# AdaLN block on one core: the out-projection in halves of 256 tokens, the MLP's first tile opened by its high parts, a table load and modulation columns placed otherwise

## What is computed

```
mod = silu(c) @ wmod          # six sets of columns: sa, ca, ga, sb, cb, gb
h = layernorm(x) * (1 + ca) + sa
x = x + ga * attention_block(h)   # RMS norm, q/k/v, rope, 32 heads of 8, causal softmax
                                  # inside blocks of 128 tokens, out-projection + residual,
                                  # RMS norm, silu(gate) * value, down-projection + residual
h = layernorm(x) * (1 + cb) + sb
x = x + gb * ffn(h)               # gated FFN of 704 with the top 2 of 8 LoRA experts
```

## Time and profile before

| | |
|---|---|
| profiled execution | 675.88 us |
| its span, first to last instruction | 674.0 us |
| PE busy | 627.5 us (93%) |
| PEld busy | 419.7 us (62%) |
| DVE busy | 408.1 us (61%) |
| ACT busy | 316.1 us (47%) |
| POOL busy | 196.5 us (29%) |
| mean granted TensorE clock | 0.968 of full |

### The profile page before, as it was taken

One profiled execution on the slowest core, in us unless ns is written; L12 is line 12 of the kernel. 1 busy time (PEld: TensorE's weight loads), 2 busy tenths in 40 slices (PEclk: granted clock), 3 DMA queues, 4 the chain that ended last, 5 costly groups with the idle time before them and its releaser, 6 DMA issues.

```text
span 674.0 us, 13925 instructions
## 1 busy us (share of the span) xinstructions
PE 627.5 (93%) x5784; PEld 419.7 (62%) x5784; DVE 408.1 (61%) x623; ACT 316.1 (47%) x478; POOL 196.5 (29%) x264
## 2 busy tenths in 40 slices
PE   5779999999999999999999998999999999969996
PEld 3645566577864666667774565766785565637772
DVE  2895644677467653668557564468647654447554
ACT  3736463356444355257444345437543544417441
POOL 1156640024016670033015662023103773000000
PEclk8689999999999999999999999999999999978997
DMA  8644000034022000025012100004102100000000
GB/s 329 227 121 132 3 3 1 1 79 110 1 62 94 2 2 2 1 51 138 1 32 64 63 3 2 1 14 123 53 1 63 64 2 2 1 0 1 1 2 31
DMA packets 16456, 31.77 MB, mean 47 GB/s; under 512 B 5060, under 2 KB 5828, under 8 KB 16260
## 3 DMA queue, kind: packets, MB, share of 16 engines
q1 hardware_dynamic: 14856, 27.98, 13.8%
q0 software_dynamic: 1152, 2.36, 1.3%
q10 hardware_dynamic: 384, 0.52, 0.3%
HBM read 12.99 MB, written 2.10 MB: 22 GB/s over the span
## 4 chain that ended last, share of the span: by engine, by line
PE 69%; DVE 13%; ACT 7%; SPq 4%; issue 4%; DMA 1%; POOL 0%; DVEq 0%; ACTq 0%; POOLq 0%
PE bank L1623 8%; PE bank L1533 7%; PE bank L1429 5%; PE bank L1425 5%; PE bank L1426 5%; SPq L409 4%; PE bank L1695 4%; PE bank L1561 3%; PE bank L1595 3%; PE bank L1790 3%; PE bank L1569 3%; PE bank L1792 3%; PE bank L1791 2%; PE bank L1659 2%; PE bank L1816 2%
## 5 line engine op out<-in xcount | busy, mean ns | idle before, releaser
L1142 DVE TENSOR_REDUCE neg_max<-bank 128x8 f32<-128x1024 f32 x64 | 77.6, 1223 | 45.7 <-PE bank L1561 45.2
L1332 DVE TENSOR_TENSOR arena<-arena,bank 128x512 f32<-128x512 f32 (+1 forms) x72 | 49.5, 688 | 72.5 <-ACT arena L864 70.7
L1425 PE MATMUL bank<-n_hi,w_lo 128*128 128x512 f32 x200 | 86.5, 433 | 6.4 <-ACT n_hi L829 3.0
L1533 PE MATMUL bank<-mask 128*128 128x512 bf16 x256 | 78.5, 389 | 5.0 <-ACT n_hi L679 2.2
L1429 PE MATMUL bank<-n_lo,w_hi 128*128 128x512 f32 x200 | 81.4, 407 | 0.7
L864 ACT ACTIVATE arena<-bank 128x512 f32<-128x512 f32 (+1 forms) x72 | 43.0, 597 | 82.7 <-PE bank L1792 47.7
L1426 PE MATMUL bank<-n_hi,w_hi 128*128 128x512 f32 x200 | 80.3, 402 | 0.0
L803 ACT ACTIVATE tile_f<-bank 128x1024 f32<-128x1024 f32 x56 | 57.2, 1025 | 32.6 <-PE bank L1595 32.0
L581 POOL TENSOR_SCALAR arena_r<-q_st,const 100x512 fp32r<-100x512 f32 x96 | 65.2, 693 | 0.0
L560 POOL TENSOR_TENSOR k_wide<-n_lo,head_of 128x512 fp32r<-128x512 f32 x30 | 32.4, 1084 | 104.9 <-DMA n_lo<-k_st 104.9
L534 POOL TENSOR_TENSOR tile_f<-tile_f,const 128x512 f32<-128x512 f32 x16 | 22.2, 1392 | 138.6 <-ACT tile_f L715 138.6
(11 more groups left out here) (177 smaller groups left out, 1182.2 us busy)
## 6 DMA issues: line engine op xcount, KB each, us to landing
q_st<-arena_r SPq DMA_DIRECT2D x96, 64.0 KB, 2.1
k_st<-arena_r SPq DMA_DIRECT2D x52, 64.0 KB, 2.0
k_st<-arena_r POOLq DMA_DIRECT2D x36, 64.0 KB, 2.3
h_next<-in_x SPq DMA_DIRECT2D x4, 512.0 KB, 3.7
tile_f<-in_x SPq DMA_DIRECT2D x4, 512.0 KB, 4.9
out<-arena SPq DMA_DIRECT2D x4, 512.0 KB, 2.6
n_lo<-k_st SPq DMA_DIRECT2D x24, 64.0 KB, 2.0
n_hi<-q_st SPq DMA_DIRECT2D x24, 64.0 KB, 2.0
```

Of the source, the lines that this page charges most:

```text
L1142: nc.vector.tensor_reduce(neg_max[:, 2 * a:2 * a + 2, MROW:KS], slot(("s1", n)).rearrange("p a (h s) -> p a h s", s=P), AX_X, ALU.max, neg ...
L1332: nc.vector.tensor_tensor(pair_tmp[n % 2][0:width], silu_out[n % 2][0:width], up, ALU.mult)\
L1425: nc.tensor.matmul(to, wl[:, at], n_hi[:, kt, :], start=kt == 0, stop=False)
L1533: nc.tensor.matmul(to, mask[:, 0, :], mask[:, which:which + 1, :].broadcast_to([P, GH, P]), start=True, stop=False)
```

## The change

The out-projection is done in two halves of 256 tokens, in the order tile 0 half 0, tile 0 half 1, tile 1 half 0, tile 1 half 1, with 16 instructions in four banks (0 and 1, then 2 and 5); the first two groups wait for units 0 to 3, the third for units 4 and 5, the last for all. VectorE adds in four pieces of 256 tokens. The next row's second squared means move behind the out-projection, and VectorE's `variance` behind the low parts; ScalarE's squares for the MLP wait for these means, since both use the same tile. The first `up` step takes all products with high inputs for both outputs first and then those with low inputs. ScalarE loads the Exp table at the end of the feed-forward part. The four spreads of the queries are all tensor_scalars. The copies of modulation columns go and all readers take their columns from `mod_all`. In the prologue VectorE takes the second unit's maxima before the last low rope, and GpSimd waits for that low rope before it begins unit 1.

```diff
-        mod = sb("mod", [P, 6 * KT])
-        front_mod = sb("front_mod", [P, 2 * KT])
+        begun = sb("begun", [P, 1])
...
-        o_proj = signal("o_proj", KT)
+        o_proj = signal("o_proj", 2 * KT)
...
+        def columns(row, c):
+            return mod_all[:, c * KT:(c + 1) * KT, row:row + 1].rearrange("p c b -> p (c b)")
+
+        def out_bank(half, t):
+            return bank[:, ((0, 1), (2, 5))[half][t], 0:S // 2]
@@ GpSimd: spread_queries and the prologue @@
-                nc.gpsimd.tensor_tensor(q_ex[u % 2][0:KS, :, 0, :], src,
-                                        con("head")[0:KS, 0:1].unsqueeze(2).broadcast_to([KS, GQ, P]), ALU.mult)
-                for hh in range(1, GH):
+                for hh in range(GH):
                     last = nc.gpsimd.tensor_scalar(q_ex[u % 2][0:KS, :, hh, :], src,
                                                   con("head")[0:KS, hh:hh + 1], 1.0, ALU.mult, ALU.mult)
...
             spread_keys(0, 2, 0)
+            pool.wait_ge(rope_lo.sem, 4)
             unit_begun(0, 1, 0)
@@ ScalarE: row_steps @@
+                if not last:
+                    act.wait_ge(front.square_mean.sem, front.square_mean.count(row, 2, 1))
                 squares(rest, 0, h)
                 deviation(rest, row, 0, 0)
...
                 product_high(len(FF_STEPS) - 1)
                 if not last:
+                    nc.scalar.preload_act_table(ACT.Exp)
                     for u in range(AHEAD):
                         max_to_rows(row, u, 1)
@@ VectorE: row_steps @@
-                nc.vector.tensor_copy(mod[:], mod_all[:, :, bass.ds(row, 1)].rearrange("p c b -> p (c b)"))\
-                    .then_inc(mod_row.sem, 1)
...
-                            front_modulation(row, 1)
...
-                if not is_last:
-                    variance(1, row)
 
                 dve.wait_ge(h_moved.sem, h_moved.count(row, 1))
-                for t in range(KT):
-                    dve.wait_ge(o_proj.sem, o_proj.count(row, t + 1))
-                    nc.vector.tensor_tensor(h[:, t, :], h[:, t, :], bank[:, t, :], ALU.add).then_inc(x1_ready.sem, 1)
+                for half in range(2):
+                    tokens = slice(half * S // 2, (half + 1) * S // 2)
+                    for t in range(KT):
+                        dve.wait_ge(o_proj.sem, o_proj.count(row, half * KT + t + 1))
+                        last = nc.vector.tensor_tensor(h[:, t, tokens], h[:, t, tokens], out_bank(half, t), ALU.add)
+                        if half:
+                            last.then_inc(x1_ready.sem, 1)
 
...
+                if not is_last:
+                    variance(1, row)
                 inverse(rest, row, 0, 0)
@@ VectorE: prologue @@
             second_keys()
+            unit_max(0, 1, 0)
             rope_low(0, 3, 0)
-            unit_max(0, 1, 0)
             chunk_low(2)
@@ TensorE: row_steps @@
-                        elif u == 7:
-                            mean_squares(front, row, 1, 1)
...
-                for kt in range(KT):
-                    pe.wait_ge(ctx_done.sem, ctx_done.count(row, (kt + 1) * BLOCKS))
+                for kt, units, half in ((0, BLOCKS, 0), (0, BLOCKS, 1), (1, BLOCKS + BLOCKS // 2, 0), (1, UNITS, 1)):
+                    pe.wait_ge(ctx_done.sem, ctx_done.count(row, units))
                     for t in range(KT):
-                        last = nc.tensor.matmul(bank[:, t, :], plain("o")[:, kt * D + t * P:kt * D + (t + 1) * P],
-                                                ctx_n[:, kt, :], start=kt == 0, stop=kt == KT - 1)
+                        last = nc.tensor.matmul(out_bank(half, t), plain("o")[:, kt * D + t * P:kt * D + (t + 1) * P],
+                                                ctx_n[:, kt, half * S // 2:(half + 1) * S // 2], start=kt == 0,
+                                                stop=kt == KT - 1)
                         if kt == KT - 1:
                             last.then_inc(o_proj.sem, 1)
+                if not is_last:
+                    mean_squares(front, row, 1, 1)
+
+                def first_up():
+                    wh, wl = hi_lo("up")
+                    at = [[slice(kt * 2 * INTER + part * INTER, kt * 2 * INTER + part * INTER + P)
+                           for part in range(2)] for kt in range(KT)]
+                    to = [bank[:, up_bank(0, part), :] for part in range(2)]
+                    for kt in range(KT):
+                        pe.wait_ge(rest.n_hi_ready.sem, rest.n_hi_ready.count(row, kt + 1))
+                        for part in range(2):
+                            nc.tensor.matmul(to[part], wl[:, at[kt][part]], n_hi[:, kt, :], start=kt == 0, stop=False,
+                                             skip_group_check=True)
+                            nc.tensor.matmul(to[part], wh[:, at[kt][part]], n_hi[:, kt, :], start=False, stop=False,
+                                             skip_group_check=True)
+                    for kt in range(KT):
+                        pe.wait_ge(rest.n_lo_ready.sem, rest.n_lo_ready.count(row, kt + 1))
+                        for part in range(2):
+                            last = nc.tensor.matmul(to[part], wh[:, at[kt][part]], n_lo[:, kt, :], start=False,
+                                                    stop=kt == KT - 1, skip_group_check=True)
+                    return last
```

More of the change, by code:

```diff
@@ L692, in deviation, with shift @@
                     .then_inc(norm.std_ready.sem, 1)
-            def shift(norm, row, ahead, to, src, columns):
+            def shift(norm, row, ahead, to, src, shifts):
                 for t in range(KT):
                     act.wait_ge(norm.scaled.sem, norm.scaled.count(row, t + 1, ahead))
-                    last = nc.scalar.activation(to[:, t, :], src[:, t, :], ACT.Identity, bias=columns[:, t:t + 1])
+                    last = nc.scalar.activation(to[:, t, :], src[:, t, :], ACT.Identity, bias=shifts[:, t:t + 1])
                 last.then_inc(norm.shifted.sem, 1)
@@ L705, in front_squares @@
                 else:
-                    shift(front, row, ahead, h_next, h_next, front_mod[:, 0:KT])
+                    shift(front, row, ahead, h_next, h_next, columns(row + ahead, 0))
                 squares(front, n, h_next)
@@ L735, in second_norm_highs @@
                     nc.scalar.activation(n_hi[:, t, :], xc[:, t, :], ACT.Identity,
-                                         bias=mod[:, 3 * KT + t:3 * KT + t + 1]).then_inc(rest.n_hi_ready.sem, 1)
+                                         bias=columns(row, 3)[:, t:t + 1]).then_inc(rest.n_hi_ready.sem, 1)
             def second_norm_shift(row):
@@ L742, in second_norm_shift @@
                     last = nc.scalar.activation(xc[:, t, :], xc[:, t, :], ACT.Identity,
-                                                bias=mod[:, 3 * KT + t:3 * KT + t + 1])
+                                                bias=columns(row, 3)[:, t:t + 1])
                 last.then_inc(rest.shifted.sem, 1)
@@ L1073, in variance @@
                     .then_inc(front.std_ready.sem, 1)
-            def front_modulation(row, ahead):
-                nc.vector.tensor_copy(front_mod[:], mod_all[:, 0:2 * KT, bass.ds(row + ahead, 1)]
-                                      .rearrange("p c b -> p (c b)")).then_inc(front_mod_ready.sem, 1)
             def front_scale(row, ahead):
-                dve.wait_ge(front_mod_ready.sem, front_mod_ready.count(row, 1, ahead))
-                scale(front, row, 0, ahead, h_next, h_next, front_mod[:, KT:2 * KT], front.scaled)
+                scale(front, row, 0, ahead, h_next, h_next, columns(row + ahead, 1), front.scaled)
             def front_rms(row, ahead):
@@ L1123, in front_rope @@
                 rope_add(row, 0, 1)
-                scale(rest, row, 1, 0, xc, xc, mod[:, 4 * KT:5 * KT], rest.scaled)
+                scale(rest, row, 1, 0, xc, xc, columns(row, 4), rest.scaled)
                 rope_low(row, 0, 1)
@@ L1383, in _ @@
             front_columns()
-            front_modulation(0, 0)
             inverse(front, 0, 0, 0)
```

30 lines of the change are left out of this document (13 added, 17 removed).

## The result

The changed kernel takes 665.65 us (median of four runs, 665.0 to 667.4), beside 675.59 us for the kernel before on the same chip: ratio 0.9864, 95% interval 0.9848 to 0.9880, or 9.9 us less by the medians and 9.2 by the ratio. Forecast were 4.8 to 5 us less (670.8, range 668.0 to 673.5). The sign was right; the size forecast was about half of the measured one, and one of the places, the feed-forward part, had been put at 0. The profiled execution took 665.03 us, its span is 663.2 us (674.0 before), its mean granted clock 0.978 (0.968).

The account below looks back on a forecast made before the run. TensorE sets the time (69% of the chain), except where a row's work passes singly through other engines. Junction 3.5 + row starts 0.75 + columns 0 + prologue 0.75 = 5.0 us off 675.9, stated as 670.8, range 668.0 to 673.5.

Parts of the forecast that it names:

- Columns in place: 0: Modulation columns read without copies: worth 0, with bounds of 0.3 us gained and 0.3 lost.
- Together 1.07 us in each of the three rows: Junction between attention and MLP, rows with a successor: 0.65 - 0.06 + 0.48 = 1.07 us gained in each.
- I take 0.25 a row: Start of three rows: Exp load ahead (0.13) and first spread as tensor_scalar (0.10); 0.75 us in all, bounds 0 and 1.2.
- the prologue's 0.75: Prologue: four tensor_scalar spreads save 0.39 us and the later low rope 0.38; 0.75 taken, bounds 0.4 and 1.3.
- the clock of the last row: Last row: moving everything some 5 us earlier can shift a low-clock stretch either way by 1 us; left unsigned.
- Mechanism of the junction: After attention: 16 instructions 0.231 us apart, statistic behind them, `up` pair 3.0 instead of 3.48; 3.5 us over four rows.
- Rival (c): Out-projection: exposed weight loads of 0.19 us on 16 instructions cost 10.6 us in all, giving 681.4, slower; 4%.
- The 0.65 by which the first x1 was to come earlier: Junction, row 0: first x1 tile ends at 104.87 instead of about 105.52, ScalarE's high parts earlier with it.
- the bound 0.4: Start of a row: upper bound of 0.4 us a row if the first scores also came earlier.
- rival (a): Prologue: clock returns to the higher level a step earlier, 1.7 us more gained, 669.1; 20%.
- (b): Downstream of the junction: its gain is taken back, in full 674.4 or half 672.6; 7% each.
- (d): Change not doing what it says: Exp load stays at row start or halves wait for all contexts; 671.5 to 673; 5%.

Follow-up runs that it names:

- e1: Kernel before with the junction's three edits alone (out-projection in halves, moved statistic, first `up` by high parts): 669.1 against 674.62 us, 0.9917.
- e5: Kernel before with the Exp table loaded ahead and all four query spreads as tensor_scalars, without the prologue's new order: 672.32 against 673.8 us, 0.9974.
- e6: Kernel before with the modulation columns read in place, nothing else: 673.0 against 673.8 us, 0.9984.
- e9: Kernel before with only the next row's second squared means moved behind the whole out-projection, first `up` order kept: 671.54 against 674.04 us, 0.9954.
- e10: Kernel after with the out-projection and its additions whole again: 665.3 us against 674.04 for the kernel before, 0.9865.
- e2: Kernel before with the four query spreads as tensor_scalars and the prologue's new order: 673.41 against 674.62 us, 0.9981.
- e3: Kernel before with only the Exp table loaded at the end of the feed-forward part: 674.57 against 674.62 us, 0.9998.
- e13: Kernel after with the two copies of modulation columns back: 665.75 us against 674.42 for the kernel before, 0.9869.
- e14: Kernel after with the out-projection whole and fill matmuls in the last row, 3 of them before the last down-projection: 662.48 against 674.42 us, 0.9822.
- the repeat: Kernel after, unchanged, profiled and timed again in another session: 665.45 us against 674.62 for the kernel before, 0.9868.
- the control: Kernel after with VectorE setting the fill tile at the start but no fill matmul: 666.47 us against 674.04 for the kernel before, 0.9886.

## Why the prediction was wrong in size

The steps that failed are terms of the sum. "Columns in place: 0", with nothing for the feed-forward part, measured 1.3 to 1.45 us there. "Together 1.07 us in each of the three rows" measured 2.06 in row 2. "I take 0.25 a row" measured 0.39, the prologue's 0.75 measured 1.26 and 2.31, and the clock of the last row, left out, gave 0.3 to 0.6. The runs with parts of the change say the same in times: by their ratios e1 gave 5.6 us (3.5 said), e5 1.8 (1.1 said for its parts, 0.75 and the 0.39 of the spreads) and e6 1.1 (0 said). They leave out only the prologue's order, and make 8.5 together beside the 8.9 to 9.2 of the whole.

- **Mechanism of the junction: right.** 0.228 us apart (0.231 said), pair 2.99 (3.0 said), rows 0 and 1 1.18 and 1.21 (1.07 said), last row 0.39 (0.30 said). The rule of the Trainium skill's page "TensorE: Matmul & The Clock Gate", section "Part 3: Packing small matmuls — row/col tiling", that loads to the same row group are exposed, does not hold here: 16 instructions with a load each took 3.72 us, eight took 3.67 to 3.70. The prediction left out that the same section also lets a load into the background weight buffer go ahead; which buffer a load went to, the traces do not show. Rival (c) falls.
- **Its parts were in the sum, under a heading that hid them.** The 0.65 by which the first x1 was to come earlier is 0.82 for the statistic moved away less 0.17 for the halves. By e9 and e10 the move is worth 0.80 and the halves -0.11, and the pair's order 0.46. So the sum itself said that the halves lose, and I did not draw from it that the out-projection should stay whole.
- **"Together 1.07 us in each of the three rows" failed in row 2.** I read row 0 and multiplied by three; row 2 held an interruption of 0.69 us. It gave 0.85 more than rows 0 and 1, 0.99 more than said. A look at each of the three rows of the kernel before would have shown it.
- **"I take 0.25 a row" failed: 0.39.** I priced the load at 0.13 and the spread at 0.10 as if they added. e2 and e3 show 0 and 0.12 each alone and e5 0.37 to 0.40 together; the bound 0.4 was in the text, for the earlier first scores, and that is what came.
- **"Columns in place: 0" failed:** I looked for a cost in the operations that read the columns and there is none, but matmuls of the feed-forward part are spaced 4 to 5 ns closer, 0.2 us a row (e6, e13). The bound of 0.3 in all was too narrow. The part as a whole gave 1.3 to 1.45. Row 0's rest is open: the profile before has a slow DMA issue of 1.54 us in SyncE's queue in it (157.69), but e10 and e14, with the columns in place, take 60.35 and 60.55 there.
- **The prologue term was right in its two parts, and too small for the whole.** The spreads became 0.90 shorter (0.77 said), and e2 and e5 lie 0.7 below the mean of the profiles without the edit. With the whole change it was 1.26 and 2.31. The rest of the scatter is the issue pause near 17 us, 1.41 before, 2.56 after, 1.34 in the repeat, which no edit aims at, and the clock: rival (a), the clock back sooner, came in both (0.92 and 1.00 where it was 0.50). It was priced at 1.7; in the repeat, whose pause is as long as before's, 1.56 beyond the 0.75 came. In e13 the clock is 1.00 in both stretches of the earlier trace rows and the pause 2.04, and the first contexts come at 53.32, 1.6 earlier than before.
- **The clock was left out of the sum as unsigned.** In the last row it gave 0.3 to 0.6, and at the end 1.8 or nothing, by the execution. So 1.3 + 0.4 + 1.4 + 0.5 (junction, row starts, feed-forward part, prologue) = 3.6 us are terms of mine that were too small, and the remaining 2.2 of the 5.8 by which the profiles differ more than my 5.0 are the last row and the tail. Of these the tail's 1.8 is chance: the repeat does not have it.
- **Rivals (b) and (d) did not come.** Nothing was given back: the marks only ever move apart. No table load stands before Exp in rows 1 to 3.
- The range failed because all unknowns were bounded one by one near their middle values, and four of them came out on one side.

## What to carry to other kernels

When a term is "so much a row", read the place in every row of the trace before, since one of three was different. When two waits end at nearly the same time, price them together; tests of one alone show little. And when an order is changed in several ways at once, test each: here the edit with the most code (the halves) was worth a loss of 0.11 us a row, while the move of one statistic made most of the junction's gain.

## What was not expected of the hardware

- The matmuls between the waits of the last row's second norm ran at the lower clock in the profiles before and after (2.07 us for the eight 128-column instructions, 1.16 with fills), and 19 otherwise useless matmuls in TensorE's waits there took the stretch of 590 to 600 us from 0.66 to 1.00. With those before the last down-projection the kernel became some 3 us faster (663.41 against the control's 666.47).
- The place of the low stretches differs between executions of one program: the last four matmuls took 1.98 or 3.78 us. With it the tail takes 6.5 (after) or 8.3 us (repeat), so a difference of that size between two profiles is no evidence by itself.
- TensorE's list is interrupted without a wait behind the same instruction, the 53rd of 64, in the profiles of three programs (before, e3, e5: 0.69, 0.55 and 0.69 us in row 2), and not in two others whose TensorE work is equal there (e2, e6).
- The same matmuls start 0.229 or 0.233 us apart at the same granted clock, by an edit that leaves these instructions alone, though it moves the tiles that they read (e6, e13).
- Reading a one-column operand with a stride of 4 elements instead of from a dense copy cost nothing that shows: a scaled operation of VectorE (128x512) takes 0.744 us before and in e6.
